# Graph transformer layers on one core: table work first, not last, in each tile's place of the joint pass

## The reference

```python
k = typed_linear(x, ntype, Wk); q = typed_linear(x, ntype, Wq); v = typed_linear(x, ntype, Wv)
kw = typed_linear_heads(k[src], etype, att)            # 32x32 per head and edge type
a = sum(kw * q[dst], -1) * pri[:, etype].T / sqrt(32)
w = softmax of a over the edges of one dst
m = typed_linear_heads(v[src], etype, msg) * w
h = segment_sum(m, dst)
h = typed_linear(h, ntype, Wa)
alpha = sigmoid(skip)[ntype]
x = h * alpha + x * (1 - alpha)
```

## Time and profile before

| | |
|---|---|
| median of 3 runs | 6516.59 us (6512.33 to 6521.16) |
| profiled execution | 6516.66 us, span 6514.9 us |
| PE busy | 4628.8 us, 71% of the span |
| DVE busy | 4972.8 us, 76% |
| ACT busy | 4070.1 us, 62% |
| POOL busy | 4223.8 us, 65% |
| granted TensorE clock, mean | 0.845 of full speed |
| the four joint passes | begin near 1300, 2579, 3860 and 5140 us, some 170 us each |
| the first layer's table stage | some 60 to 190 us |

### The profile page before, as it was taken

One profiled execution on the slowest core, in us unless ns is written; L12 is line 12 of the kernel. 1 busy time (PEld: TensorE's weight loads), 2 busy tenths in 40 slices (PEclk: granted clock), 3 DMA queues, 4 the chain that ended last, 5 costly groups with the idle time before them and its releaser, 6 DMA issues.

```text
span 6514.9 us, 170550 instructions
## 1 busy us (share of the span) xinstructions
PE 4628.8 (71%) x33358; PEld 3951.0 (61%) x33359; DVE 4972.8 (76%) x14638; ACT 4070.1 (62%) x10772; POOL 4223.8 (65%) x4629
## 2 busy tenths in 40 slices
PE   7766666696666666976666679766666786666665
PEld 6665555575565555765655567655665676555553
DVE  6777777787777777777777777777777778777776
ACT  3467666645666665456666654666666547666665
POOL 1577777526777774277777743777777347777773
PEclk9888888798888888988888879788888898888887
DMA  6433333353333333533333335333333353333331
GB/s 223 140 108 107 107 107 108 91 235 104 107 107 107 107 107 101 230 99 107 107 107 107 107 120 210 100 107 106 107 107 106 139 191 102 107 107 106 106 108 54
DMA packets 306187, 783.84 MB, mean 120 GB/s; under 512 B 105775, under 2 KB 138900, under 8 KB 305012
## 3 DMA queue, kind: packets, MB, share of 16 engines
q0 software_dynamic: 196560, 537.00, 28.8%
q1 hardware_dynamic: 109092, 241.62, 9.9%
HBM read 573.87 MB, written 195.88 MB: 118 GB/s over the span
## 4 chain that ended last, share of the span: by engine, by line
PE 29%; DVEq 21%; issue 18%; DVE 17%; POOL 7%; DMA 4%; ACT 2%; ACTq 1%; POOLq 0%; SPq 0%
POOL rows L563 7%; DVEq L1446 7%; DVEq L1436 6%; PE ps L701 5%; PE ps L879 4%; PE ps L863 4%; DMA rows<-table,idx_now 3%; PE ps L884 3%; PE ps L725 3%; DVEq L286 3%; PE ps L712 3%; PE ps L695 2%; DVE prod L1430 2%; PE ps L878 1%; DVE wmsg L1408 1%
## 5 line engine op out<-in xcount | busy, mean ns | idle before, releaser
L563 POOL DMA_INDIRECT rows<-table,idx_now x4095 | 3965.9, 968 | 1389.4 <-issue 1145.7
L998 ACT ACTIVATE prod<-iota_n,dloc 128x128 bf16<-128x128 f32 x6240 | 1983.6, 389 | 21.0 <-issue 1.8
L878 PE MATMUL ps<-zeros,identb 128*128 128x132 bf16 x2080 | 516.5, 248 | 1517.8 <-DVE wmsg L1408 1248.1
L863 PE MATMUL ps<-qn,ohT 128*128 x8320 | 1429.9, 325 | 81.3 <-issue 61.7
L863 PEld LDWEIGHTS ps<-qn,ohT 128*128 128x128 f32 x8320 | 1252.1, 230 | 161.6 <-issue 143.1
L878 PEld LDWEIGHTS ps<-zeros,identb 128*128 128x128 bf16 x2080 | 225.1, 108 | 1690.6 <-issue 1571.4
L1003 ACT ACTIVATE ohf<-prod,ones 128x512 f32<-128x512 bf16 x1040 | 750.7, 722 | 731.4 <-PE ps L884 652.2
L879 PE MATMUL ps<-wmsg,ohf 128*128 128x132 f32 x4160 | 1122.8, 359 | 0.0
L1404 DVE TENSOR_TENSOR wmsg<-rows,weight 128x512 f32<-128x512 f32 x1040 | 724.1, 696 | 341.0 <-issue 309.4
L884 PE MATMUL ps<-wmsg,ohf 128*128 128x132 f32 x4160 | 976.2, 323 | 0.0
L1430 DVE TENSOR_TENSOR prod<-ps,rows 128x512 f32<-128x512 f32 x1040 | 716.5, 689 | 270.8 <-DMA rows<-table,idx_now 134.7
(11 more groups left out here) (166 smaller groups left out, 5474.2 us busy)
## 6 DMA issues: line engine op xcount, KB each, us to landing
table<-rows SPq DMA_DIRECT2D x245, 768.0 KB, 3.3
stage<-table SPq DMA_DIRECT2D x8320, 1.0 KB
rows<-table,idx_now POOLq DMA_INDIRECT x4095
rows<-in_node_type SPq DMA_DIRECT2D x5, 2613.0 KB, 10.5
rows<-stage SPq DMA_DIRECT2D x65, 128.0 KB
rows<-in_node_type SPq DMA_DIRECT2D x5, 512.0 KB, 4.2
out<-h SPq DMA_DIRECT2D x3, 704.0 KB
idx_row<-row_of SPq DMA_DIRECT2D x65, 0.5 KB
```

The costliest lines, as they stand in the source:

```text
L563: pool.indirect_dma_start(out=rows[:, slot, j, :], out_offset=None, in_=table, in_offset=bass.IndirectOffsetOnAxis(ap=idx_now[:, half, c:c ...
L863: last = pe.matmul(ps[:, 2 + b, j * P:(j + 1) * P], ohT[:, b, j, :], qn[:, at(ts[j]), :].rearrange("p a c -> p (a c)"), start=True, stop=True)
L878: pe.matmul(bank[:, AW:2 * AW], identb[:], zeros[:], start=True, stop=True)
L998: act.activation(squares[:, turn % 2, j * P:(j + 1) * P], iota_n[:], ACT.Square, bias=dloc[:, at(4 * q + j)], scale=-1.0)
```

## The change

In `between_`, on three engines, the work for tile t-2 (PE `products`, ACT `v_half`, DVE `k_half`) moves from the end of the body of t to its beginning. No instruction, buffer or semaphore is added or taken away, and POOL and SP keep their lists. The rest of each body keeps its order, and so do the closing lines of the last body.

```diff
@@ tensor engine, between_.body(t, b, pair) @@
                         sums(0, 0)
                         sums(1, 1)
                         out_product(0, 0)
+                    if not is_first(t, 2):
+                        products(l + 1, t - 2, b)
                     if not beyond(t + 2, TILES):
                         sums(t + 2, b)
                     if not is_last(t, TILES):
...
                     turn_h(t, b, 3)
                     if not is_first(t):
                         projections(t - 1, 1 - b)
-                    if not is_first(t, 2):
-                        products(l + 1, t - 2, b)
                     if is_last(t, TILES):
@@ scalar engine, between_.body @@
+                    if not is_first(t, 2):
+                        v_half(l + 1, t - 2, b, pair - 1)
                     if not beyond(t + 2, TILES):
                         sum_copy(l, t + 2, b, 1)
                     h_copy(l + 1, t, 3)
                     if not is_first(t):
                         kv_copy(l + 1, t - 1, 1 - b, 2)
-                    if not is_first(t, 2):
-                        v_half(l + 1, t - 2, b, pair - 1)
@@ vector engine, between_.body @@
+                    if not is_first(t, 2):
+                        k_half(l + 1, t - 2, b, pair - 1)
                     if not is_last(t, TILES):
                         mixed(l, t + 1, 0)
                     masked(l + 1, t, b)
-                    if not is_first(t, 2):
-                        k_half(l + 1, t - 2, b, pair - 1)
```

## The result

| | before | changed |
|---|---|---|
| median | 6518.88 us (4 runs, 6512.33 to 6522.35) | 6626.47 us (4 runs, 6622.41 to 6629.30) |
| profiled span | 6514.9 us | 6627.5 us |
| ratio | | 1.0166, 95% interval 1.0148 to 1.0183 |

The change makes the kernel 108 us slower. The forecast was 6639.5, 123 us slower, with a range of 6608 to 6668.

The account below looks back on a forecast made before the run. PE's own work was taken to bound the joint pass; 31.3 us for 46 longer steps, -1.6 at the start and +1.0 at the end gave 30.7 a pass, times 4 123 us, so 6639.5 us, range 6608 to 6668.

Parts of the forecast that it names:

- PE is the bound of the joint pass: Joint pass before the change: PE's own work fills the 3.22 us steady tile, with no idle time before its rows.
- The circle: Repeating order of steps per tile on each engine; unchanged, except products follow the projections of their own tile.
- The size of the wait: PE before products (L725), waiting for copy L914: 0.69 us more per tile, 3.91 instead of 3.22.
- the hand-over from ACT to PE: From the end of copy L914 to the start of products L725: 0.14 us, taken from L904 in the first layer.
- the hand-over from PE to ACT: From the modelled end of the v projections to the start of copy L914: 0.11 us, called plain latency.
- Nothing below 0.55 is possible: Lower bound of the added wait per tile, with a 0.00 hand-over, as long as products need the copy.
- restart cost of the matmuls: Extra matmul time after PE's stall: nothing added; as a rival 0.12 us a tile, +22 us, 6662, chance 15%.
- Nothing else ends later: Walk through the new circle: DVE, ACT, POOL and stores all have room, DVE gaining 0.8 us of idle time.
- The start, -1.6: Start of each pass: products of tile 0 start right after the first copy, near 1312.1 instead of 1313.7 us.
- The end, +1.0: Products 46 to last eviction's end: 8.9 instead of 7.64 us, +1.3, less part of a saved store wait.
- Rival C: Joint pass not slower or faster: DVE sets the pace at 3.08 us a tile, 6483; 6% together with no change.
- Rival A: Only part of the wait shows, through a 0.00 hand-over or waits hidden in PE's busy time: 6614 or 6588; 17%.

Follow-up runs that it names:

- two lengthened kernels: Two spare 256-column copies put ahead of the copy of kT and vT: on the changed kernel 6734.44 us, on the kernel before 6517.66 us.
- half copy: Changed kernel with the copy of kT and vT cut into two copies of 128 columns, each with its own semaphore: 6606.23 us, ratio 1.0139.
- middle kernel: Table work of tile t-2 moved to the middle of the body on PE, DVE and ACT, against the changed kernel's place at the start: 6573.62 us, ratio 1.0094.

## Why the prediction was right, and what was off

- PE is the bound of the joint pass: right. The kernel before shows one wait of 0.2 us in 150 us of PE's list. Small waits do hide in the modelled busy time. In the loop's turns three steps in a row (two in the first turn) are longer than 3.22 us, up to 3.37, eleven of the 46 in all, together some 1.1 us a pass. The last of a group of three, in the kernel before:

```profile
1366.65 0.81 PE L695 MATMUL ps<-wa,rows 128*128 128x384 f32 x2
1366.71 0.55 POOL L588 COPY rows<-h 128x128 f32 x1 [1.89 <-DVE h L1259]
...
1367.36 0.14 PEld L689 LDWEIGHTS ps<-ident,rows 128*128 128x128 f32 x1 [0.52 <-POOLq L590]
1367.36 0.33 PE L689 MATMUL ps<-ident,rows 128*128 128x128 f32 x1
```

The transpose of h (L689) starts 0.71 behind L695 instead of 0.64, held by POOL's h, and the projections (L701) start 0.17 behind it instead of 0.11. The prediction put what the mean step holds above the steady tile down to the loop's branches. The step in which PE passes the branch takes 3.22 like the others; the long ones come after it.
- The circle is the same and one tile tighter, and products now wait for the copy of their own tile: right. Between the first products and those of tile 46 there are 46 waits, all at L725 for L914. The two lengthened kernels show that it is this copy: +111 us in one order, nothing in the other.
- The size of the wait, 0.69 us a tile in my sum: too big. Measured 3.83 - 3.22 = 0.61 in a tile of the loop, over the pass 3.808 - 3.229 = 0.58. The main mis-sized term is the hand-over from ACT to PE. I took 0.14 from the earlier trace rows, "the same engine pair before the same instruction". It was 0.06. The copy was another: behind L904 the hand-over was 0.14 in the kernel with PE's move alone as well (1404.80 to 1404.94), and behind L914 and the half copy 0.05 to 0.06. That is 0.08 x 184 = 15 us.
- The second mis-sized term is the hand-over from PE to ACT, 0.11, read in a body of the loop. In the bodies written out it is 0.04, and some 13 of the 46 steps are of that kind: 0.07 x 13 x 4, some 4 us. Together the steps were put some 19 us too high (31.3 against 26.6 a pass). Start and end of the pass, put 0.8 us a pass too low, took 3 of it back. That leaves the miss of 15, 123 against 108, so a part of the closeness is two errors of opposite sign.
- "Nothing below 0.55 is possible" did not hold either: where the bodies are written out a tile takes 3.75 - 3.22 = 0.53 more. The mean of the pass, 0.58, lies between my bounds.
- No restart cost of the matmuls: right. From the restarted L725 to L692 are 0.87 us, against 0.86 before, and ACT starts to empty its results 1.09 behind the start of L725, against 1.13. The Trainium skill, page "TensorE: Matmul & The Clock Gate", section "LDWEIGHTS (loading the stationary operand)", gives a load of 128 columns 128 / 1.2 = 107 ns. My estimate from it, another 0.1 us a tile for a load that can't be pulled ahead, does not show in this trace.
- Nothing else ends later: right, for this order. DVE idled in front of L1237, 36.3 us over 46 waits of the first pass or 0.79 each, where I had said about 0.8; ACT came to L914 in time (idle 0.89), the stores had room (208 GB/s). That ACT's slack mattered, the middle kernel showed by using it up.
- The start, -1.6, was -1.3. The first copy L914 came 8.8 us behind the first `mixed` and not 8.4 as before: the granted clock rose later, and the v projections before it took 1.48 us instead of 1.05. Up to there PE's list is the same in both kernels, so this is not worked by the new order.
- The end, +1.0, was +1.5. Of this, 0.3 is a slip in the sum: the chain of 8.9 us held no wait for a store, and I took the saved store wait off it once more. Further, the projections of the last tile waited 0.58 us for `masked`, which now stands behind one eviction more, a wait I had put on the copy with 0.6.
- The clock stayed at 1.00 between 1340 and 1380 us, with PE waiting 0.54 us in each step: right. It stayed there in the lengthened kernel too, with waits of 1.09.
- Rival C, DVE as the bound, fell: in the changed kernel DVE has 28.56 busy of 40 us and PE waits. Rival A's reason, hidden waits of PE for POOL that the new circle takes away, is seen: the long steps of the first point are gone, all steps of the changed loop but one take 3.82 or 3.83. It is worth 1.1 us a pass, and the sum held it already, since it starts from the mean step of before. Its number, 6614, came about as near as mine, 6639.5, since the hand-over was short.

## What to carry to other kernels

In a software pipeline written as a loop body, draw the list as a circle before judging a move: moving a piece from the end to the start changes no neighbour on the circle, only the tile it works on, and so the depth of the pipeline. Then look at the pair of neighbours where producer and consumer are now the same tile, and sum what the hand-over through the other engine takes (here 0.11 + 0.37 + 0.06 us in the loop) against the work that stands between them (here none); and check what is queued on the other engine ahead of the step that hands over. Take hand-over times from a row with the same copy, not only with the same engines, and from both kinds of bodies where some are written out and some run in a loop.

## What the runs showed of the hardware

- The hand-over from ACT to a waiting PE differed from copy to copy: 0.05 to 0.06 us behind the copy of 128 or 256 columns in the joint pass, 0.14 behind L904, which writes 384 columns in pieces of 32. In the queries it was 0.00 behind a copy of 128 columns. Why is open: size and pattern differ together, and L904 was tried in no other form.
- The hand-over from PE's modelled end to ACT was 0.04 us in written-out bodies and 0.11 in the loop, where a register instruction of 0.04 stands in ACT's queue before the copy.
- A 128-row product directly behind the 32-row products of L725 took about 0.1 us more until the next one (0.75 against 0.64 for L695). Placed between, the transpose L692 takes 0.17 instead of 0.11. So the small transpose pays only a part of it.
- ACT copies of 256 columns in a row start 0.27 us apart, though a single one takes 0.37; two of 128 start 0.16 apart and take 0.27 each. Cut in two, the copy ends 0.06 us later (0.16 + 0.27 = 0.43 against 0.37) and hands over its first half 0.10 us earlier.
- With PE's move alone the granted clock was 1.00 between 1404 and 1410 us and 0.50, the lower of the two levels (1.2 GHz), between 1412 and 1414; before it fell PE had waited 2.41 us before one tile's products and 2.08 before the next. A stretch with both levels in it reads between them, 0.91 in the window below. With the DVE and ACT parts alone, where PE waits 1.61 and 0.82 us in one tile, the windows above read 0.80 and 0.71. With waits of 1.09 us in steps of 4.37 it stayed at 1.00, the upper level (2.4 GHz).

```profile
1400.00:1440.00 40.00, 26.18 (x231) 20.56 (x224) 19.17 (x56) 12.16 (x35) 6.67 (x14) 0.91 0.34 138
...
1404.00:1410.00 6.00, 3.29 (x32) 2.59 (x32) 3.32 (x10) 2.08 (x6) 1.00 (x3) 1.00 0.32 131
...
1412.00:1414.00 2.00, 2.00 (x9) 1.54 (x8) 0.64 (x2) 0.27 (x1) 0.00 (x0) 0.50 0.59 237
```

(windows, kernel with PE's move alone)
